# A recurrent mixer on one core: the order of the convolution's taps and the addition that completes y

## The reference, cut to what matters

```python
proj = einsum('bld,pd->blp', hidden, W_in)             # gate | x,B,C | dt
hbc  = silu(conv1d(proj[x,B,C], conv_w, K=4) + conv_b)  # 4 taps, causal, per channel
Y_diag = einsum(scores * Lmat, x * dt)                 # inside a chunk
Y_off  = einsum(C, prev_states, state_decay)           # from the carried state
y = Y_diag + Y_off + D * x
g = y * silu(gate)
out = (g * rsqrt(mean(g * g) + eps) * norm_weight) @ W_out
```

## Time and profile before

| what | us |
|---|---|
| median of three runs | 2948.74 |
| the profiled execution | 2949.92 |
| its span | 2948.2 |
| PE busy | 2591.4 (88%) |
| DVE busy | 2095.3 (71%) |
| ACT busy | 1211.8 (41%) |
| POOL busy | 1139.5 (39%) |

### The profile page before, as it was taken

How to read it: one execution, slowest core, us unless ns; L and a number is a source line. 1 busy time by engine, 2 the same in 40 slices (tenths; PEclk the granted TensorE clock), 3 DMA queues, 4 the chain that set the end, 5 groups by cost and what they waited for, 6 DMA issues and landing times. The chain is left out here.

```text
span 2948.2 us, 44171 instructions
## 1 busy us (share of the span) xinstructions
PE 2591.4 (88%) x14212; PEld 1911.2 (65%) x14212; DVE 2095.3 (71%) x3431; ACT 1211.8 (41%) x2468; POOL 1139.5 (39%) x1240
## 2 busy tenths in 40 slices
PE   4894289999999999999999943999999869999993
PEld 2783278888888888888888832888888633333322
DVE  3355678888888888888888855777777664444434
ACT  1122145555555555555555521222222234444441
POOL 0251146565665656565665521455445200000000
PEclk9997589999999999999999976999999879999996
DMA  3100200000000000000000010000000031111114
GB/s 117 42 17 31 70 2 3 28 3 28 3 3 28 3 28 3 28 3 28 3 3 3 3 58 25 18 28 26 24 24 24 25 99 36 37 37 37 37 27 96
DMA packets 82365, 83.65 MB, mean 28 GB/s; under 512 B 25120, under 2 KB 71040, under 8 KB 79904
## 3 DMA queue, kind: packets, MB, share of 16 engines
q1 hardware_dynamic: 80672, 81.48, 9.4%
q10 hardware_dynamic: 1536, 0.20, 0.0%
HBM read 62.42 MB, written 16.78 MB: 27 GB/s over the span
## 5 line engine op out<-in xcount | busy, mean ns | idle before, releaser
L734 DVE SCALAR_TENSOR_TENSOR mix_cv<-mix_pp,mix_cw,mix_cv 128x384 f32<-128x384 f32 (+4 forms) x864 | 493.0, 571 | 25.4 <-ACT mix_cv L657 4.5
L1495 DVE TENSOR_REDUCE att_tops<-att_psc 128x1 f32<-128x512 f32 (+3 forms) x384 | 202.1, 555 | 219.3 <-PE att_psc L1433 131.8
L965 POOL TENSOR_TENSOR ffn_hl<-ffn_h,ffn_hh 128x512 fp32r<-128x512 f32 x144 | 186.2, 1293 | 319.6 <-ACT ffn_hh L1023 319.6
L1470 PE MATMUL att_po<-att_pr,att_vh 128*17 128x512 f32 (+3 forms) x768 | 290.6, 489 | 0.0
L581 PEld LDWEIGHTS mix_pyd<-mix_xdt,mix_lm 128*128 128x128 f32 x2048 | 249.1, 193 | 56.7 <-issue 53.1
L1534 ACT ACTIVATE att_pr<-att_pst 128x512 f32<-128x512 f32 (+3 forms) x384 | 175.8, 489 | 250.9 <-PE att_pst L1452 247.5
L75 PE MATMUL mix_pp<-l0in_XH,mix_wx_lo 128*128 128x384 f32 (+2 forms) x576 | 238.5, 414 | 36.3 <-DVE mix_ss L723 20.2
L657 ACT ACTIVATE mix_cv<-mix_pp,mix_cb,mix_cw 128x384 f32<-128x384 f32 (+1 forms) x288 | 182.4, 633 | 210.2 <-PE mix_pp L77 210.2
L632 PE MATMUL mix_pgt<-mix_wo,mix_gt 128*128 128x256 f32 x1024 | 244.9, 382 | 2.9 <-issue 2.2
L581 PE MATMUL mix_pyd<-mix_xdt,mix_lm 128*128 128x64 f32 x2048 | 244.4, 273 | 2.5 <-DVE mix_lm L784 2.5
L520 POOL TENSOR_TENSOR mix_xdt<-mix_xtok,l_dt 128x512 f32<-128x512 f32 x128 | 133.8, 1045 | 278.8 <-ACT mix_xtok L684 278.8
(11 more groups left out here) (292 smaller groups left out, 6712.6 us busy)
## 6 DMA issues: line engine op xcount, KB each, us to landing
mix_w_raw<-in_w_in SPq DMA_DIRECT2D x8, 1280.0 KB, 5.9
ffn_raw<-in_wgu SPq DMA_DIRECT2D x56, 128.0 KB, 2.2
mix_ll<-cs SPq DMA_DIRECT2D x384, 4.0 KB
att_qs<-q SPq DMA_DIRECT2D x192, 32.0 KB
mix_wo_raw<-in_w_out SPq DMA_DIRECT2D x8, 512.0 KB, 6.7
ffn_draw<-in_wd SPq DMA_DIRECT2D x28, 128.0 KB, 2.1
q<-qkv_part SPq DMA_DIRECT2D x24, 128.0 KB, 1.9
k<-qkv_part SPq DMA_DIRECT2D x24, 128.0 KB, 1.9
```

The source lines that it names most:

```text
L734: last = dve.scalar_tensor_tensor(out, of, cw[:, g, ct, 3 - d:4 - d], out, ALU.mult, ALU.add)
L965: pool.tensor_tensor(hl[u % NH][:, :], h[u % 2][:, :], hh[u % NH][:, :].bitcast(F32), ALU.subtract).then_inc(lo_done, 1)
L1470: last = pe.matmul(po[half][0:DH + 1, q0 - half * 512:q1 - half * 512], vh[(a + 1) % 2][:, kt, :], pr[(a + 1) % 2][:, at:at + q1 - q0], st ...
L1495: dve.tensor_reduce(tops[o][:, col:col + 1], psc[g % 2][:, 0:end - c], AX.X, ALU.max).then_inc(mx_done, 1)
```

## The change

VectorE's taps of the slot's first block are put in front of the addition that completes y. They stood behind it.

```diff
                     if len(fills(c - 1)) > 1:
                         finish(fills(c - 1)[-1])
+                    if ks:
+                        taps(ks[0])
                     if 0 <= p < NC:
                         if p % CPS:
                             dve.wait_ge(t1x_done, n_off(p))
...
                         wait(dve, gt_done, p - 1)
                         wait(dve, sq_done, p - 1)
                         dve.tensor_tensor(y[o][:, :], pyd[:, :], (t1 if p % CPS else xd)[o][:, :], ALU.add).then_inc(y_done, 1)
-                    if ks:
-                        taps(ks[0])
                     if 0 <= p < NC:
                         dve.wait_ge(tg_done, p + 1)
```

## The result

The changed kernel takes 2984.44 us (median of four runs, 2982.63 to 2984.59) against 2949.17 us before (2948.06 to 2952.24). The ratio is 1.0117, with an interval of 1.0099 to 1.0134: 35 us slower.

A forecast was written before the change was run, and what follows sets the result against it. TensorE was taken to bound the mixer; delays of 2.34 us per eight pieces, times 15.4 groups, add 36 us to the median of 2948.74, forecast as 2985 us, range 2967 to 3000.

The forecast's parts named there:

- VectorE's new order: VectorE, mixer: the taps can hardly run in the addition's place, as they wait for init; idle before them above 150 us.
- The shift of z: VectorE, pieces with taps: z comes later by 0.61 us less what the taps gain; fifth piece 0.54.
- The slack: TensorE, two-block pieces: time beyond the tightest 1.90 us from z's end to the transposes (L640); 0 to 0.36.
- The delays by piece: TensorE's delay in each piece of a group of eight: 0.27, 0.24, 0.45, 0.16, 0.38, 0.38, 0.46, 0 us.
- The sum over the kernel: Mixer, 123 pieces: 2.34 us per eight pieces in 15.4 groups, 36 us slower.
- Nothing gives it back: Mixer: a TensorE delay in one piece is not made up later, since TensorE runs on without a break.
- The early squash: ScalarE's tanh and the exponential behind it come up to 0.63 us earlier; that gain ends in a wait for z.
- The addition's price: VectorE: the moved addition costs 0.61 us per piece; at a strict 0.69, 9 us more, 2994 us.
- the slack absorbs the pieces that have some: TensorE: only the third, fourth and seventh pieces pay, 2965 us; chance 0.11.
- each piece pays 0.61: VectorE becomes the bound and all 123 pieces pay in full: 75 us, 3024 us; chance 0.06.
- Faster: Earlier tanh and exponential (L693) remove TensorE's 14.1 us of waits, z not late enough to matter: 2935 us; chance 0.04.
- no change: TensorE's order absorbs the whole delay: 2949 us; chance 0.03.

## Why the prediction was right

The forecast was 2985 us, the time is 2984.44. That the two lie 0.6 apart is luck, since the runs of one kernel spread by 2 to 4 us; the agreement piece by piece, below, is not.

- **VectorE's new order.** I took it that the taps can't use the addition's place, for they wait for init. The trace after has that wait 123 times, 167.6 us (above 150 was forecast).
- **The shift of z.** For the fifth piece I had 0.54: 3.87 - 3.33 = 0.54.
- **The slack.** 1.90 from z's end to the transposes is measured as the floor, in the fifth and in all other swapped two-block pieces but the very first. The output projection never starts before z's end plus 0.10.
- **The delays by piece.** Forecast: 0.27, 0.24, 0.45, 0.16, 0.38, 0.38, 0.46, 0. Measured by the table: 0.26, 0.23, 0.46, 0.16, 0.38, 0.38, 0.47, -0.02. The sum is 2.32 for 2.34.
- **The sum over the kernel.** Forecast 36, the mixer's pieces have 34.9. The first eight pieces lost 1.87 and not 2.32. The first has no output projection that could wait for z. In the second one the taps had started 0.62 behind init (408.51, 409.13) before, so it had nothing to lose.
- **Nothing gives it back.** This holds for the whole change. It was too simple as a rule: the run with the swap in five of eight shows a return of 0.14 and 0.07 in the pieces between.
- **The early squash.** It came, as the rival had it, and ended in a wait for z, as the text had it against the rival. One reading was off: TensorE waited for that exponential in the eighth piece alone, which are the 15 times of the earlier trace rows, and not in the fourth.
- **The addition's price.** It is 0.60 to 0.61 in the rows, not 0.69. With the stricter reading of the Trainium skill ("VectorE: DVE Perf Modes", section "The DRAIN you can't avoid") the time would have been 2994, by the prediction's estimate. The trace goes with that section's exception: the next instruction starts 0.60 behind the addition's start (1564.29, 1564.89), before its 0.68 are over.

One statement was wrong. I had expected TensorE's busy time to stay. It rose by 14.6 us (1310.57 to 1325.17), and its idle time by 19.4, which together are the 34 by which I made the stretch longer. No matmul was added. The output projection's own rows have 4.5 us of it (244.9 to 249.4): behind a wait its eight matmuls show 1.97, unhindered 1.89. Most of the rest is an overlap with the matmul in front that is gone. In the fifth piece before:

```profile
1536.15 0.40 PE L563 MATMUL mix_pd<-mix_rl,mix_ll 96*128 96x256 bf16 x2
1536.38 1.89 PE L632 MATMUL mix_pgt<-mix_wo,mix_gt 128*128 128x256 f32 x8
```

and after:

```profile
1565.87 0.40 PE L563 MATMUL mix_pd<-mix_rl,mix_ll 96*128 96x256 bf16 x2
1566.40 1.97 PE L632 MATMUL mix_pgt<-mix_wo,mix_gt 128*128 128x256 f32 x8
```

Before, the output projection started 0.17 before the end of the one in front (1536.55), after it starts 0.13 behind it (1566.27). Of the delay of 0.38 only 0.13 is thus idle time in the profile; 0.17 and 0.08 are booked as work. The ends of matmuls are modelled in the profile, so this says how a stall is counted, not that TensorE did more.

The rivals: that the slack absorbs the pieces that have some fails by the table (0.26 in the first, 0.38 in the fifth). It had 2965, which the stated range from 2967 did not reach, though the text says so. That each piece pays 0.61 fails by the eighth. Faster and no change are out by the result.

## What to carry to other kernels

An idle gap in front of an instruction isn't free room for whatever stands behind it. Ask when that work's own input arrives: here the gap ended with the wait for one engine, and the other's input came at the same moment, so the short instruction that had filled the gap was what got exposed. The sign of such a swap is decided piece by piece by the distance from the moved work's input to its start, set against what the overtaken work takes, here 0.61: at 0.03 to 0.48 the swap cost, at 0.66 it was worth nothing, at 1.2 the same swap gained 8 to 9 us. Of a cost, the bounding engine feels only what goes beyond its slack: in the fifth piece z came 0.54 later, and TensorE had 0.17 of slack and lost 0.38. And an edit that lets the bounding engine run ahead must be followed into the next piece, where it may be given back.

## What the runs showed that was not expected

- TensorE's "issue" idle time in front of the output projection (11.1 us in 22 cases, before 2.2 in one) is a wait for z: in the eighth piece, and in the last one of all, it ends 0.10 behind z's end. The waits' view named z nowhere, in either kernel, though five of the seven delays came through z. The distances in the timeline showed it.
- The kernel before has some 15 us of slack to gain in VectorE's order alone: t1 in front of the output row brings it to 2932.20 us.
